# Half taps and small statistics by turns in tile 3 of a convolution block

## The reference

```
h    = group_norm(x, 32 groups)               # mean and variance over 8 channels x 56 x 56
h    = gelu(depthwise_conv_3x3(h, dw))        # zero padding, 9 taps a channel
maps = pw (2048 x 256) @ h + pw_b             # 8 maps of 256 channels, one for each direction
out  = x
for i, (dx, dy) in enumerate(8 directions):
    out += maps[i] * (roll(x, (dy, dx)) - x)
```

## Time and profile before

| | us |
|---|---|
| median of 3 runs (2212.94 to 2213.73) | 2213.64 |
| profiled execution, its own time | 2213.16 |
| its span in the profile | 2211.4 |
| TensorE matmuls busy | 2157.7 |
| VectorE busy | 2066.0 |
| GpSimd busy | 1982.2 |
| ScalarE busy | 1839.9 |

### The profile page before, as it was taken

The page is one execution under the profiler, slowest core; times in us unless marked ns, Lnnn a source line. Parts: engine busy times, 40 slices in busy tenths (PEclk is TensorE's granted clock), DMA queues, the critical chain, the costliest instruction groups (busy, mean ns, idle before and its releaser), DMA issues.

```text
span 2211.4 us, 28738 instructions
## 1 busy us (share of the span) xinstructions
PE 2157.7 (98%) x10769; PEld 2018.4 (91%) x10769; DVE 2066.0 (93%) x2234; ACT 1839.9 (83%) x2762; POOL 1982.2 (90%) x860
## 2 busy tenths in 40 slices
PE   1999999999999999999999999999999999999998
PEld 1999999999999999999999999999999999999998
DVE  7999999999999999999999999999999999999995
ACT  5979889798887988889788897988879888798775
POOL 5799899899989999899898998989989998999986
PEclk9999999999999999999999999999999999999999
DMA  6245264443725337254362644536354372543424
GB/s 183 49 80 128 48 113 99 90 103 51 155 54 106 92 61 159 34 109 100 69 141 35 124 95 81 117 51 125 84 93 99 56 157 47 109 98 53 100 34 75
DMA packets 47083, 202.13 MB, mean 91 GB/s; under 512 B 3040, under 2 KB 7136, under 8 KB 45664
## 3 DMA queue, kind: packets, MB, share of 16 engines
q0 software_dynamic: 30192, 94.97, 26.4%
q1 hardware_dynamic: 16752, 105.34, 18.4%
HBM read 104.88 MB, written 146.80 MB: 114 GB/s over the span
## 4 chain that ended last, share of the span: by engine, by line
PE 84%; DVE 11%; ACT 2%; issue 2%; DMA 0%; POOL 0%; SPq 0%; POOLq 0%; DVEq 0%; ACTq 0%
PE psum L966 84%; DVE psum L819 4%; DVE products L722 3%; ACT psum L607 1%; DVE psum L722 1%; DVE psum L828 1%; ACT psum L575 1%; DVE acc L744 1%; ACT hid L589 1%; DMA acc<-x 0%; DVE acc L784 0%; POOL hlo L337 0%; DVE mean_b L698 0%; DVE psum L699 0%; DVE fields L851 0%
## 5 line engine op out<-in xcount | busy, mean ns | idle before, releaser
L607 ACT ACTIVATE psum<-psum,bias,rstd 128x448 f32<-128x448 f32 x1792 | 1200.1, 694 | 323.3 <-PE psum L966 320.0
L966 PE MATMUL psum<-hhi,w_hi 128*128 128x448 f32 x3601 | 1301.9, 362 | 47.3 <-ACT hhi L594 45.5
L368 POOL TENSOR_TENSOR acc<-acc,products 128x896 f32<-128x896 f32 x333 | 1166.4, 3503 | 161.6 <-DVE products L722 151.5
L966 PE MATMUL psum<-hhi,w_lo 128*128 128x448 f32 x3584 | 1299.9, 363 | 0.0
L966 PE MATMUL psum<-hlo,w_hi 128*128 128x448 f32 x3584 | 1008.7, 363 | 0.3 <-POOL hlo L337 0.3
L828 DVE SCALAR_TENSOR_TENSOR psum<-xn,dw_f,psum 128x896 f32<-128x896 f32 x768 | 882.3, 1149 | 72.1 <-ACT psum L579 66.4
L966 PEld LDWEIGHTS psum<-hhi,w_hi 128*128 128x128 f32 x3601 | 676.3, 188 | 97.4 <-issue 45.5
L966 PEld LDWEIGHTS psum<-hlo,w_hi 128*128 128x128 f32 x3584 | 672.8, 188 | 45.0 <-POOL hlo L337 0.9
L966 PEld LDWEIGHTS psum<-hhi,w_lo 128*128 128x128 f32 x3584 | 673.3, 188 | 44.1
L722 DVE TENSOR_TENSOR products<-psum,fields 128x896 f32<-128x896 f32 x556 | 602.8, 1084 | 14.5 <-ACT psum L607 11.1
L337 POOL TENSOR_TENSOR hlo<-hid,hhi 128x896 fp32r<-128x896 f32 x112 | 264.7, 2364 | 12.5 <-ACT hhi L594 12.5
(11 more groups left out here) (72 smaller groups left out, 451.7 us busy)
## 6 DMA issues: line engine op xcount, KB each, us to landing
out<-acc POOLq DMA_DIRECT2D x96, 896.0 KB, 7.8
out<-x SPq DMA_DIRECT2D x16, 3136.0 KB, 12.4
xpad<-x SPq DMA_DIRECT2D x30, 1568.0 KB, 14.8
out<-acc POOLq DMA_DIRECT2D x15, 448.0 KB, 5.6
acc<-x SPq DMA_DIRECT2D x4, 784.0 KB, 6.9
xpad<-pw_t SPq DMA_DIRECT2D x1, 2048.0 KB, 12.2
out<-products SPq DMA_DIRECT2D x2, 224.0 KB, 2.0
dw_f<-dw SPq DMA_DIRECT2D x1, 9.0 KB, 8.2
```

Source lines behind the costliest of these rows:

```text
L368: nc.gpsimd.tensor_tensor(a, a, p, ALU.add).then_inc(added_s, 1)
L607: nc.scalar.activation(m, m, ACT.Identity, bias=bias[ip][:, g, d:d + 1], scale=rstd[ip][:, g:g + 1]).then_inc(biased_s, 1)
L966: last = nc.tensor.matmul(maps(n0 * UNITS + q)[:, side, x0:x1], w[:, kk, col:col + P], h_part(h, t, nl, kk)[:, x0:x1], start=s == 0, stop= ...
```

## The change

Tile 3, and only it, gets an order of its own on VectorE. The half taps become a function `half_tap`, issued singly; `tap_next` still issues two of them. Between the first products and the first kept product the order was (s a step of the statistics, h a half tap)

```diff
+            def half_tap(n0, b0, c, j, g):
+                conv, ky, kx = conv_of(n0, c), *divmod(TAPS_DVE[j], 3)
+                if j == 0:
+                    dve.wait_ge(start_s, upto(START_OF, b0, c) + (g + 1))
+                else:
+                    dve.wait_ge(tap_s, upto(TAPS_OF, b0, c) + (2 * (j - 1) + g + 1))
+                d = conv[:, g, :].rearrange("p (r c) -> p r c", c=W)
+                nc.vector.scalar_tensor_tensor(
+                    d, xn[c % 2][:, g * TR + ky:g * TR + ky + ROWS, kx:kx + W],
+                    dw_f[:, g, TAPS_DVE[j]:TAPS_DVE[j] + 1], d, ALU.mult, ALU.add).then_inc(tap_s, 1)
+
             def tap(n0, b0, c, j):
...
-                if s == SINGLE:
-                    for g in range(HALVES):
...
-                    return
...
-                    taps = iter(range(NT) if not (last and nl + 3 >= STEPS) else ())
+                    single = (nl + 3) % CSTEPS == SINGLE
+                    taps = iter(range(NT) if not single and not (last and nl + 3 >= STEPS) else ())
+                    half_taps = iter(itertools.product(range(NT), range(HALVES)) if single else ())
+
+                    def half_tap_next():
+                        for j, g in itertools.islice(half_taps, 1):
+                            half_tap(n0, b0, nl + 3, j, g)
 
                     def tap_next():
                         for j in itertools.islice(taps, 1):
                             tap(n0, b0, nl + 3, j)
+                        half_tap_next()
+                        half_tap_next()
...
-                    stats_next()
-                    stats_next()
-                    tap_next()
-                    stats_next()
-                    second_product(n0, nl)
-                    second_add(n0, nl)
-                    stats_next()
-                    tap_next()
+                    if single:
+                        stats_next()
+                        half_tap_next()
+                        stats_next()
+                        half_tap_next()
+                        stats_next()
+                        half_tap_next()
+                        second_product(n0, nl)
+                        stats_next()
+                        second_add(n0, nl)
+                        half_tap_next()
+                    else:
+                        tap_next()
+                        second_product(n0, nl)
+                        second_add(n0, nl)
+                        tap_next()
                     stats_next()
                     kept_product(n0, nl, 3)
```

More of the change, by code:

```diff
@@ L907, in body @@
                     first_product(n0, nl, 1)
+                    assert single == (t == STATS_TILE)
                     if t == STATS_TILE and not (last and par):
                         stats = iter(group_stats(b0 + par + 1))
-                    stats_next()
-                    stats_next()
-                    tap_next()
-                    stats_next()
-                    second_product(n0, nl)
-                    second_add(n0, nl)
-                    stats_next()
-                    tap_next()
+                    if single:
[14 more added lines that the diff above has]
+                        tap_next()
                     stats_next()
```

## The result

The changed kernel took 2207.2 us (median of 9 runs, 2206.72 to 2207.97) where the kernel before took 2213.45 (9 runs, 2212.34 to 2213.93): a ratio of 0.9974, 95% interval 0.9965 to 0.9983. It is 6.25 faster, with an interval of about 3.8 to 7.7; 2207.4 was forecast.

A forecast was written before the change was run, and what follows sets the result against it. TensorE was taken to set the pace, held 15 times by VectorE: 15 x 0.42 = 6.3 off the profiled 2213.16 gives 2206.9, and 0.48 for the median gives 2207.4 us; range 2206.5 to 2210.6.

The forecast's parts named there:

- TensorE's 15 holds: Tile 4, unit 2, in 15 images: TensorE's weight load waits for VectorE's last kept product of tile 3, 0.5 us each.
- the second rival: TensorE makes up for the hold by issuing matmuls faster, so there is no gain: 2213.6 us; chance 0.03.
- The 0.42: Time in us that each held image loses on TensorE, 134.86 against 134.44; over 15 images 6.3, the most to gain.
- 0.48 of lateness: Tile 4, unit 2: the weight load was due at 1073.18 and began at 1073.66, so VectorE is 0.48 us late.
- SP: Second product (unit 2) on VectorE in tile 3: to start 0.18 us later, with no more waiting for ScalarE.
- SA: Add of the second product, releasing unit 5 of tile 3: to come 0.18 us later, with 0.18 to spare.
- s4: Statistics step of two small instructions, moved between second product and its add: its 0.19 us to be covered there.
- K3: First kept product on VectorE in tile 3: to start 0.61 us earlier, at 61.56 instead of 62.17.
- K7: Last kept product of tile 3, releasing tile 4, unit 2: to end at 1073.00, leaving 0.13 us to spare.
- the tap: Third half tap, moved from behind the second product's add to before that product: 0.59 us taken away ahead of K3.
- The first rival: The wait moves to unit 5 of tile 3 because s4 costs its upper price: 2210.5 us; chance 0.09.
- The slower rival: No VectorE instruction in the new order starts before the previous ends, K3 0.81 later: 2225 us; chance 0.06.

The follow-up runs named there:

- the fourth experiment: The changed kernel with one half tap more in front of the second product in tile 3: 2214.35 us, ratio 1.0005 to the kernel before.

## Why the prediction was right

- **What bounds it.** That only TensorE's 15 holds count: the holds went, tile 4 fell to 19.24 everywhere, and the time by 6.25 where 6.3 had been worked out from 15 x 0.42. So close a match is in part luck, as the interval of the gain is almost 4 wide. TensorE made up for no hold in any of the seven kernels that have holds; no tile takes less than 19.20. That rejects the second rival. The prediction had taken 189 ns for it from the Trainium skill's page "TensorE: Matmul & The Clock Gate", section "Back-to-back issue gap". The section gives that formula for a single matmul by itself and, for a stream with weight loads, a lower figure of about 131 ns for 512 columns. The traces differ from both, with 200 ns for 448 columns.
- **The 0.42.** It was read as one term and is two. The hold is 0.39 to 0.40: 0.48 of lateness at the weight load less 0.09. Three other values of lateness bear the 0.09 out: 0.28 cost 0.19, 0.40 cost 0.32, and 0.21, in the last image of the fourth experiment, cost 0.12. The rest, 0.42 against 0.39 to 0.40 on average, is the pace of 0.207 behind some holds up to the cut: tile 4 takes 19.69 or 19.70 in images 4, 7, 11, 12 and 13 and 19.62 to 19.66 in the other ten. That is five images with 12 such matmuls, where the later expectations say six with 15. The sum came out right since it was taken from whole images.
- **The steps on VectorE.** SP 0.18 later (0.18 measured), SP to SA 1.21 (1.20), s4 covered, K3 0.61 earlier (0.63), 0.13 of room at K7 (0.14) and 0.18 at SA (0.19).
- **The parts.** The gain in lateness was put down as 0.59 for the tap, 0.19 for s4, less 0.18 (0.60; the steps laid out one by one give 0.61). Alone the tap gave 0.52, with SP 0.09 later, and s4 gave 0.21. Since 0.48 less the free 0.09 was all there was to win, the tap alone reaches the full gain, s4 alone half of it, and together they reach no more; the text did not say that one part would do.
- **The first rival** was real in its place, though not by the cause that it gave (s4 cost nothing), and 0.19 away: one half tap more, and unit 5 is held in every image. Its price stood in the forecast without the pace of 0.207, which in the fourth experiment put 0.46 on top of the hold's 0.32 in six images. (Its time, 2213.6 less 3, is 2210.6 and not 2210.5.)
- **The slower rival**, no overlap between VectorE's instructions in the new order, had nothing in it: the six starts after h1 come at 0.60, 0.10, 0.58, 0.10, 0.59 and 1.00.

## What to carry to other kernels

Where an engine that sets the pace is held by another at one place of a period, work out the lateness there, and look upstream for idle time of the other engine that independent work can be moved into; what counts is only the lateness taken away up to what the holder has, so one move can be worth all and the next nothing. Price the instruction that the move delays by what it releases, with its room. A gap between an instruction and one that needs it can take small independent work for nothing, as the 0.2 between SP and SA took the two of s4. And when a median hides two kinds of runs, read the list.

## What the hardware showed that had not been expected

- TensorE has two paces for the same pairs of weight load and matmul of 448 columns at a granted clock of 1.00: 0.200 and 0.207. The second was seen behind some holds and not behind others, and behind the first matmuls of four of the twelve traces. It lasted 72 matmuls in image 7 of the fourth experiment, until the cut matmul, and to the end of the kernel, some six and a half images, where there was no cut. It made the traced run about 26 longer (2238.92 against 2212 to 2214); the longest run of that kernel, untraced, is 59 longer.
- The cut matmul costs 0.04 by itself (19.24 against 19.20), where the pace is 0.200.
- A weight load can be up to about 0.09 late at no cost to the matmuls. This is an estimate from the four pairs above, 0.48 and 0.39, 0.40 and 0.32, 0.28 and 0.19, 0.21 and 0.12; no run had a lateness under 0.09.
